# A fused adapter, attention, rotation and mixture-of-experts block on one core: the second norm ahead of the routing, the routing beside the feed-forward products, a reordered opening, and sums moved to ScalarE

## The reference, cut to what matters

```python
B, S, D = 32, 64, 256                      # 2048 tokens
# 1 adapter
hid = gelu(x @ down_W.T + down_b)                       # 64 wide
hid = where(valid, hid @ expert_W[dom].T + expert_b[dom], hid) + domain_emb[dom]
x = layernorm(hid @ up_W.T + up_b + x) * gamma + beta
# 2 attention and feed-forward
x = layernorm(x) * (1 + scale) + shift                  # scale, shift = silu(sin_emb(t)) @ W_ada + b_ada
x = x + softmax(mask(q k^T / 4 + bias)) v @ Wo + bo     # 16 heads of 16
x = x + gelu2((layernorm(x) * g2 + beta2) @ W1 + b1) @ W2 + b2     # 1024 wide
# 3 rotation of pairs by theta and phi of the batch row
# 4 style and mixture of experts
h = layernorm(x) * ln_g + ln_b
h = (h - mean_over_s) * rsqrt(var_over_s) * gamma + beta           # gamma, beta from the subject's style net
gates, idx = top2(softmax(h @ router_w))                # 8 experts, gates normed to sum 1
return x + sum_of_two(gate * (relu(h @ w1[e] + b1[e]) @ w2[e] + b2[e]))
```

## Time and profile before

| | us |
|---|---|
| median of 3 runs | 686.25 (685.91 to 686.96) |
| the profiled execution, its own time | 689.78 |
| its span | 687.9 |
| TensorE, VectorE, ScalarE, GpSimd busy | 557.8, 468.5, 297.2, 226.5 |
| share of the chain that ended last: TensorE, VectorE | 53%, 24% |

### The profile page before, as it was taken

How to read it: one execution, slowest core, us unless ns; L and a number is a source line. 1 busy time by engine, 2 the same in 40 slices (tenths; PEclk the granted TensorE clock), 3 DMA queues, 4 the chain that set the end, 5 groups by cost and what they waited for, 6 DMA issues and landing times.

```text
span 687.9 us, 15375 instructions
## 1 busy us (share of the span) xinstructions
PE 557.8 (81%) x4840; PEld 413.9 (60%) x4841; DVE 468.5 (68%) x1308; ACT 297.2 (43%) x616; POOL 226.5 (33%) x137
## 2 busy tenths in 40 slices
PE   3719576999597997769949399999789999999992
PEld 1616355558385484654838248676567778777771
DVE  5573796689979979883897935886454646474751
ACT  1615542642564425535243232666364444353540
POOL 0412553207714238133370422122612313122222
PEclk9999668999988999989978599999999999999996
DMA  8583451913066451466606576773532322222220
GB/s 288 127 203 124 156 158 56 226 32 123 1 170 160 131 184 63 130 149 227 200 1 244 210 253 232 274 260 49 171 48 41 50 40 42 33 48 38 43 42 0
DMA packets 41176, 86.49 MB, mean 126 GB/s; under 512 B 7321, under 2 KB 31810, under 8 KB 37026
## 3 DMA queue, kind: packets, MB, share of 16 engines
q1 hardware_dynamic: 21744, 56.77, 24.1%
q0 software_dynamic: 8352, 16.99, 13.4%
q10 hardware_dynamic: 11026, 12.02, 5.9%
HBM read 57.23 MB, written 29.44 MB: 126 GB/s over the span
## 4 chain that ended last, share of the span: by engine, by line
PE 53%; DVE 24%; issue 7%; ACT 5%; DMA 5%; ACTq 3%; POOL 2%; SPq 0%; DVEq 0%; POOLq 0%
PE bank L1918 8%; PE bank L1743 6%; PE bank L1907 5%; PE bank L1909 5%; PE bank L1908 4%; PE bank L1919 4%; PE bank L1642 3%; PE bank L1707 2%; PE bank L1723 2%; DMA stage<-in_moe_w 2%; PE bank L1752 2%; PE bank L1697 2%; ACTq L855 2%; DVE stats L1038 2%; DVE sc_sum L1127 2%
## 5 line engine op out<-in xcount | busy, mean ns | idle before, releaser
L1907 PE MATMUL bank<-xs_f,w_moe 128*128 128x128 f16 x624 | 123.3, 221 | 11.0 <-issue 6.6
L1909 PE MATMUL bank<-xs_f,w_moe 128*128 128x128 f16 x624 | 123.6, 221 | 2.7 <-issue 2.7
L867 ACT ACTIVATE stage<-bank,cols 128x128 f32<-128x128 f32 x312 | 88.3, 373 | 81.7 <-PE bank L1909 39.3
L1908 PE MATMUL bank<-xs_f,w_moe 128*128 128x128 f16 x624 | 122.8, 220 | 0.7 <-issue 0.7
L646 POOL DMA_INDIRECT out_x<-x_kept,ids x39 | 62.6, 1606 | 171.3 <-DVE x_kept L1511 122.3
L1907 PEld LDWEIGHTS bank<-xs_f,w_moe 128*128 x624 | 61.1, 98 | 47.0 <-issue 19.2
L1918 PE MATMUL bank<-w_moe,split 128*128 x208 | 79.3, 384 | 0.6
L1908 PEld LDWEIGHTS bank<-xs_f,w_moe 128*128 x624 | 61.4, 98 | 3.6 <-issue 0.8
L1909 PEld LDWEIGHTS bank<-xs_f,w_moe 128*128 x624 | 61.2, 98 | 3.5 <-issue 2.5
L1743 PE MATMUL bank<-w_moe 128*128 128x512 f32 x128 | 59.6, 627 | 3.2 <-ACT w_moe L745 3.2
L1005 DVE SCALAR_TENSOR_TENSOR split<-stage,split 128x2048 f16<-128x2048 f32 x16 | 41.4, 2585 | 30.4 <-ACT split L685 30.4
(11 more groups left out here) (273 smaller groups left out, 1186.8 us busy)
## 6 DMA issues: line engine op xcount, KB each, us to landing
stage<-in_moe_w SPq DMA_DIRECT2D x16, 1024.0 KB, 7.7
w_split<-split SPq DMA_DIRECT2D x16, 1024.0 KB, 4.9
w_moe<-w_split SPq DMA_DIRECT2D x8, 2048.0 KB
w_moe<-in_bias POOLq DMA_DIRECT2D x8, 1024.0 KB, 11.6
xs<-dispatched ACTq DMA_DIRECT2D x41, 130.0 KB
w_moe<-in_x_f SPq DMA_DIRECT2D x4, 512.0 KB, 7.1
w_moe<-in_x_t SPq DMA_DIRECT2D x4, 512.0 KB, 8.0
out_x<-x4b ACTq DMA_DIRECT2D x4, 512.0 KB
```

The lines of the kernel that those rows point to most:

```text
L867: ins = act.activation(h32[j][:, f, :], bank[banks + g][:, P * (f % 4):P * (f % 4) + P], ACT.Relu, bias=moe_b1[:, bass.ds(e, 1), f], scale ...
L1907: pe.matmul(o, hi, xs_f[j][:, k, :], start=(k == 0), stop=False)
L1908: pe.matmul(o, hi, xs_f[j][:, KD + k, :], start=False, stop=False)
L1909: mm = pe.matmul(o, lo, xs_f[j][:, k, :], start=False, stop=(k == KD - 1))
```

## The change

1. Routing a turn later. At the end of a turn TensorE and VectorE no longer run `rank`, `turn_gates`, `expert_biases` and `choose` to `accumulate`. VectorE runs `norm2(c + 1)` right after `style_apply`. The routing of chunk c - 1 runs at the top of turn c, before `norms`; TensorE's three steps stand between the parts of `feed_forward1(c)`, and ScalarE's exponential (`token_gates(c - 1)`) between its second and third activation. `dispatch(c - 1)` moves to the top of GpSimd's turn. The routing of chunk 2 runs beside chunk 3's products, ahead of the plan for the expert stage. Banks are dealt out anew, and the logits are copied by ScalarE (`logits`).
2. Sums to ScalarE. `bo` is added by ScalarE in `keep` (two activations with a bias), the output projection is copied out by ScalarE (`take_x2`), and both halves of `values` are ScalarE's. VectorE's `values` and `residual` are gone.
3. Loop order. `split_low(c + 1, 0)` comes after `sums(0)`; on ScalarE `exponentials(c + 1, 1)` comes after `keys(c + 2)`, and `split_high(c + 1, 2)` after `values`, ahead of `feed_forward_in`; `turn1(c + 2)` comes after the first half of `feed_forward2`, and in turn 1 `scores(c + 1, 1)` after the second.
4. Opening. `ints` and `cols` are loaded first and VectorE starts on them; the other tables come from ScalarE's queue; chunk 0's domain matrices are loaded half by SP and half by ScalarE; `w_qkv` and `main` are issued only after the time angles' activations. The style net runs between the query and key products of chunk 0; `down_projection(1)` and `domain_experts(1)` come before the scores are done; the masks of chunk 1 after both contexts of chunk 0.
5. `x4` is one buffer for all chunks, and `accumulate` adds to it in place.

```diff
 LEFT = 2 + TURNS * STEPS
 ENTRIES = LEFT + STEPS
 DIGIT = E
-ADAPTER_BANKS = ((2, 3, 2), (2, 3, 2), (7, 6, 6), (7, 6, 6))
+ADAPTER_BANKS = ((2, 3, 2), (6, 7, 6), (7, 6, 6), (7, 6, 6))
 TURN1_BANK = (0, 0, 4, 4)
 TURN3_BANK = (4, 4, 4, 6)
-ROUTE_BANK = (0, 0, 0, 3)
-ROWS_BANK = (4, 4, 4, 6)
+LOGIT_BANK = (5, 5, 5, 3)
+COUNT_BANK = 3
+ROWS_BANK = (2, 2, 2, 6)
 GATES_BANK = (2, 2, 2, 3)
 B2_BANK = (2, 2, 2, 6)
...
-    load_x(0)
-    load_x(1)
+    load_features(0)
+    sp.dma_start(down_w[:], t["down_w"].rearrange("(k p) a -> p k a", p=P)).then_inc(down_in, 16)
+    load_experts(0, CB // 2)
+    load_tokens(0)
+    load_features(1)
+    load_experts(1)
     load_part(0, 0)
+    load_tokens(1)
...
     for c in range(NCH - 1):
         residual(c)
-        confirm(c)
+        if c > 0:
+            dispatch(c - 1, range(TT))
         less_maximum(c + 1, 0)
         if c + 2 < NCH:
             shift_norm(c + 2)
@@ -629,12 +629,13 @@
         probabilities(c + 1, 0)
         rotate_odd(c)
         probabilities(c + 1, 1)
+        confirm(c)
         if c + 3 < NCH:
             select(c + 3)
         if c + 2 < NCH:
             add_bias(c + 2)
-        dispatch(c, range(TT))
     residual(NCH - 1)
+    dispatch(NCH - 2, range(TT))
     confirm(NCH - 1)
...
+    for dst, src in early:
+        act.dma_start(dst[:], src).then_inc(early_in, 16)
+    for dst, src in of_adapter:
+        act.dma_start(dst[:], src).then_inc(adapter_in, 16)
...
+
+    act.wait_ge(dom_ready, 1)
+    _, chosen = nc.values_load_multi_w_load_instructions(
+        dom_at[0:1, CB // 2:CB], engines=[mybir.EngineType.Activation], min_val=0, max_val=NDOM - 1)
+    for b in range(CB // 2):
+        act.dma_start(w_raw[:, CB // 2 + b, :],
+                      t["exp_w"][bass.ds(chosen[b], 1), :, :].rearrange("e a o -> a (e o)")
+                      ).then_inc(w_raw_in.sem, 16)
+    act.dma_start(w_ada[:], t["w_ada"].rearrange("(k p) n -> p k n", p=P)).then_inc(ada_in, 16)
+    for dst, src in of_style:
+        act.dma_start(dst[:], src).then_inc(style_in, 16)
...
+    act.dma_start(w_qkv[:], t["w_qkv"].rearrange("(k p) n -> p k n", p=P)).then_inc(qkv_in, 16)
+    for dst, src in main:
+        act.dma_start(dst[:], src).then_inc(main_in, 16)
+
+    act.wait_ge(mask_ready, 1)
+    for u in range(2):
+        mask(0, u)
+    split_high(0, 0)
+    queries(0)
+    keys(0)
+    split_high(0, 1)
+    values(0)
+    hidden(1)
...
-    act.wait_ge(mask_ready, 1)
-    for u in range(2):
-        mask(0, u)
-    act.wait_ge(main_in, N_MAIN)
-    split_high(0, 0)
-    queries(0)
-    keys(0)
-    values(0)
     keep(0)
-    split_high(0, 1)
+    split_high(0, 2)
     exponentials(0, 0)
-    hidden(1)
     exponentials(0, 1)
-    split_high(0, 2)
     context(0, 0)
+    context(0, 1)
     mask(1, 0)
-    context(0, 1)
+    take_x2(0)
     mask(1, 1)
-    split_high(0, 3)
     queries(1)
     keys(1)
     keep(1)
 
     hidden(2)
     values(1)
+    split_high(0, 3)
     for c in range(NCH - 1):
         feed_forward_in(c)
+        feed_forward(c, range(2))
         if c > 0:
-            feed_forward(c, range(5))
+            token_gates(c - 1)
+        feed_forward(c, range(2, KF))
+        if c > 0:
+            store(c - 1)
             split_high(c, 3)
-            feed_forward(c, range(5, KF))
-        else:
-            feed_forward(c, range(KF))
+        exponentials(c + 1, 0)
         split_high(c + 1, 0)
-        exponentials(c + 1, 0)
-        split_high(c + 1, 1)
-        exponentials(c + 1, 1)
         if c + 2 < NCH:
             queries(c + 2)
             keys(c + 2)
+        exponentials(c + 1, 1)
         context(c + 1, 0)
+        split_high(c + 1, 1)
         norm3(c)
         context(c + 1, 1)
         if c + 2 < NCH:
-            for u in range(2):
-                mask(c + 2, u)
-        split_high(c + 1, 2)
-        token_gates(c)
+            mask(c + 2, 0)
+        take_x2(c + 1)
+        if c + 2 < NCH:
+            mask(c + 2, 1)
+        logits(c)
         rows(c)
         if c + 3 < NCH:
             hidden(c + 3)
         if c + 2 < NCH:
             keep(c + 2)
             values(c + 2)
-        store(c)
+        split_high(c + 1, 2)
...
-    dve.wait_ge(cond_in, N_COND)
+    dve.memset(v_bd[:], 0.0).then_inc(zeroed, 1)
+    step(dve.tensor_scalar(bq4[:], bq[:], 0.25, None, ALU.mult))
+    step(dve.tensor_tensor(bkp[:], bk[:].unsqueeze(2).broadcast_to([P, KD, 2]),
+                           parity[:].unsqueeze(1).broadcast_to([P, KD, 2]), ALU.mult))
+    dve.wait_ge(early_in, N_EARLY)
+    dve.tensor_copy(ident16[:], ident[:]).then_inc(zeroed, 1)
+    dve.tensor_copy(lower16[:], lower[:]).then_inc(zeroed, 1)
+    dve.wait_ge(setup_pe, 1)
+    step(dve.tensor_copy(add_o[:], bank[7][0:A, 0:B]))
+    dve.wait_ge(zeroed, 9)
+    hidden()
+    dve.wait_ge(adapter_in, N_ADAPTER)
+    residual()
+    norms()
+    dve.wait_ge(setup_pe, 2)
+    for m in range(2 * KD):
+        step(dve.tensor_scalar(ada[:, m, :], bank[5][:, B * m:B * m + B], b_ada[:, m:m + 1],
+                               1.0 if m < KD else 0.0, ALU.add, ALU.add))
+    dve.drain().then_inc(cond_ready, 1)
+    scale_norm()
...
+    split_low(0, 0)
...
-    dve.wait_ge(setup_pe, 6)
+    split_low(0, 1)
...
+    scores(0)
+    hidden, adapter_residual, norms = adapter(1)
+    hidden()
+    scores(1)
+    adapter_residual()
+    sums(0)
...
+    sums(1)
     norms()
+    split_low(0, 2)
+    stages = second_half(0)
+    norm2, *_ = stages
+    scale_norm, *_ = attention(1)
     scale_norm()
...
-    split_low(0, 0)
-    values()
-    scores(0)
-    split_low(0, 1)
-    scores(1)
-    hidden, adapter_residual, norms = adapter(1)
-    hidden()
-    sums(0)
-    adapter_residual()
-    sums(1)
-    split_low(0, 2)
-    norms()
-    stages = second_half(0)
-    residual, norm2, *_ = stages
-    residual()
-    scale_norm, *_ = attention(1)
-    scale_norm()
-    split_low(0, 3)
...
     for c in range(NCH - 1):
-        _, values, scores, sums = attention(c + 1)
-        (_, _, second_residual, rotate, norm3, style_stats, style_scale, style_apply, choose,
-         token_gates, find_place, copy_gates, accumulate, fill_rows) = stages
-        values()
+        _, scores, sums = attention(c + 1)
+        if c + 2 < NCH:
+            hidden, adapter_residual, norms = adapter(c + 2)
+            hidden()
+        if c == 0:
+            split_low(0, 3)
+        else:
+            fill_rows()
+            choose()
+            token_gates()
+            find_place()
+            copy_gates()
+            split_low(c, 2)
         if c + 2 < NCH:
             adapter_residual()
+        if c > 0:
+            accumulate()
+        if c + 2 < NCH:
             norms()
         if c > 0:
             split_low(c, 3)
...
-        split_low(c + 1, 0)
         scores(1)
         sums(0)
+        split_low(c + 1, 0)
+        (_, second_residual, rotate, norm3, style_stats, style_scale, style_apply, choose,
+         token_gates, find_place, copy_gates, accumulate, fill_rows) = stages
...
-        residual, norm2, *_ = stages
-        residual()
-        choose()
-        token_gates()
-        find_place()
-        copy_gates()
-        fill_rows()
+        norm2, *_ = stages
         norm2()
-        accumulate()
-        if c + 3 < NCH:
-            hidden, adapter_residual, norms = adapter(c + 3)
-            hidden()
-        split_low(c + 1, 2)
...
+    split_low(NCH - 1, 2)
+    fill_rows()
+    choose()
+    token_gates()
+    find_place()
+    copy_gates()
     plan_early()
+    accumulate()
...
+    pe.wait_ge(early_in, N_EARLY)
+    pe.wait_ge(setup, SETUP_DOM)
+    pe.matmul(bank[7][0:A, 0:B], dom_emb[:], hot_dom[:], start=True, stop=False)
+    pe.matmul(bank[7][0:A, 0:B], exp_b[:], hot_val[:], start=False, stop=True).then_inc(setup_pe, 1)
+    domain_experts(0)
+    pe.wait_ge(zeroed, 9)
+    pe.wait_ge(adapter_in, N_ADAPTER)
+    up_projection(0)
+    pe.wait_ge(ada_in, 16)
     pe.wait_ge(setup_act, 4)
...
-    domain_experts(0)
-    pe.wait_ge(zeroed, 9)
-    up_projection(0)
     turn1(0)
     pe.wait_ge(cond_ready, 1)
-    pe.wait_ge(main_in, N_MAIN)
-    queries(0)
-    keys(0)
+    pe.wait_ge(qkv_in, 16)
+    pe.wait_ge(x1_ready.sem, x1_ready.of(0, 2))
+    project(0, 0, wq, q_done, range(0, 1))
+    pe.wait_ge(style_in, N_STYLE)
+    pe.wait_ge(setup, SETUP_SUB)
+    pe.matmul(bank[4][0:SE, 0:B], subj_emb[:], hot_sub[:], start=True, stop=True).then_inc(setup_pe, 1)
+    project(0, 0, wq, q_done, range(1, KD))
+    pe.wait_ge(setup, SETUP_SE)
+    pe.matmul(bank[5][0:SH, 0:B], hyp_w1[:], se[:], start=True, stop=True).then_inc(setup_pe, 1)
+    project(0, 2, wk, k_done, range(0, 1))
+    pe.wait_ge(setup, SETUP_SE + 1)
+    pe.matmul(bank[6][0:SH, 0:B], hyp_w2[:], hyp1[:], start=True, stop=True).then_inc(setup_pe, 1)
+    project(0, 2, wk, k_done, range(1, KD))
+    pe.wait_ge(setup, SETUP_SE + 2)
```

(38 more changed lines are left out.)

214 lines of the change are left out of this document (93 added, 121 removed).

## The result

| | before | after |
|---|---|---|
| first comparison, median of 4 runs each | 686.4 | 680.9 (676.6 to 682.1) |
| a profiled execution, own time (span) | 689.78 (687.9) | 682.14 (680.3) |

The ratio is 0.991 (95% interval 0.989 to 0.993), 5.5 us gained where 12.4 were forecast. That is not all of the result: the same changed kernel, measured twice more later, stood at 1.003 (1.000 to 1.007) and 1.005 (1.001 to 1.009) of the kernel before, which took 692.1 and 691.6 beside it. The gain was there in one measurement of three. The ratios leave out runs more than 1.5% above the kernel's fastest; over all twelve runs of each, the two later medians are 697.8 and 698.8, which is 5.8 and 7.2 above the kernel before.

The account below looks back on a forecast made before the run. Stages bound it: TensorE waits for VectorE's routing and norm, the two alternate in S to O, and the opening is a lone chain. 10.8 + 20.0 - 16.5 - 1.9 = 12.4 us gained, median 686.25 to 674, range 665 to 684.

Parts of the forecast that it names:

- O to S: From a turn's first routing product (O) to the next turn's first feed-forward product (S): 20.0 us gained over three turns.
- the stop of 2.3 ahead of `turn_gates`: In chunks 1 to 3, TensorE stops 2.3 us within the feed-forward products, waiting for the gates.
- that rival: A table load costs twice its 1.28 us: gates and stop come 1.3 later, 3.9 in three chunks; 678, chance 0.03.
- The opening: From the start to chunk 0's first feed-forward product: 10.8 us gained (9.9 + 2.9 - 2.0), bounds 6 and 14.
- S to O: From a turn's first feed-forward product to its first routing product, three times: 16.5 us lost together, 10 to 20.
- the handover: From chunk 3's first feed-forward product to the first expert product, 31.09 us before: 1.9 lost, 0 to 4.
- Step (b): Turns 1 and 2: routing beside feed-forward products stops TensorE 2.3 us and puts VectorE's norms 10 later, 5 to 6 absorbed.
- (c): In S to O, `split_low(c + 1, 0)` now lies ahead of the third norm: 2.5 us in the sum.
- (a): Turn 0's S to O, without routing: `exponentials(1, 1)` waits for ScalarE's keys, `sums(1)` 3.5 us later, 1 to 4.
- Expert stage: From the first expert product to the end of the span, 263.0 us: taken as untouched and costed at nothing.
- the cases at 680 and 681: 680: the opening gains 5 instead of 10.8, chance 0.19. 681: the norm ahead gains 2 instead of 5.5 each, 0.09.
- the slower one: Routing beside the products holds VectorE until each S to O grows more than it saves, by 11.5: 692, chance 0.07.

Follow-up runs that it names:

- routing-back kernel: Changed kernel with all engines' routing steps back between the router and the next chunk's second norm, other changes kept: 1.005 of before.
- fillers: Changed kernel with ten useless products (128x512 or 128x128) in TensorE's stop ahead of `turn_gates`, turns 1 and 2: 1.010 and 1.009 of before.
- e6: Changed kernel with the gap's exponential ahead of the first `feed_forward` activation (chunk 3: behind the first): 0.987 of before.
- e12: Changed kernel with the gates' activation ahead of the first `feed_forward` activation and computed in the same table as these: 0.979 of before.
- e5: Changed kernel with `split_low(c + 1, 0)` back ahead of `scores(1)` and `split_high(c + 1, 0)` ahead of the exponential: 1.001 of before.
- e2: Changed kernel with `turn_gates` two feed-forward parts later and `expert_biases` one part later in TensorE's queue: 1.004 of before.
- e7: Changed kernel with ten useless 128x128 products in TensorE's stop ahead of `turn_gates` in turns 1 and 2: 1.009 of before.

## Why the prediction was wrong in size

**Right.** Direction and range of the first measurement; the bottleneck by stages; the opening's chain (first query product 39.65, forecast 41; chunk 1's 101.52, forecast 105; first feed-forward product 119.89, forecast 125); O to S, 20.6 of 20.0, with 13.7, 11.7 and 8.8 where 14, 12 and 9 stood; the two loads inside the products and the stop of 2.3 ahead of `turn_gates` (2.27, 2.26, 2.26). On the load itself the Trainium skill ("ScalarE: Activation LUTs", What ACT_TABLE_LOAD costs) has 1.28 and a drain of 1.38 behind it. The trace has the 1.28, with the exponential 1.29 after the load's start, and no drain; that rival is out.

**The opening** gave 15.9 instead of 10.8, more than its upper bound of 14. Both first parts were shorter than I took: chunk 0's queries 11.1 earlier (9.9), the stretch to chunk 1's 5.3 shorter (2.9), and ScalarE's longer part cost 0.5 and not 2.0. (The 4.4 of the masks and the shift should have been 4.5, from 2.46 and 2.09.)

**The term that failed is S to O with the handover**: 18.4 lost in the sum, 31.3 in the trace. The routing-back kernel splits it.

- *Step (b) and the handover, the routing beside the products: 9.9 forecast (4.5, 3.5, 1.9, with 2.5 for (c) taken off the 7 and 6), 17.0 measured (5.6, 5.0, 6.4).* I placed the second activation's end at S + 4.35 and the gates at S + 7.8, with every part at 1.74, the full clock's price. In turn 1 it was S + 6.1 and S + 9.5: behind the pause ahead of S (1.56, 4.57, 0.87 in the three) the clock was already halved, and in turn 1 and chunk 3 it halved again behind the stop. `feed_forward1` with its routing steps took 21.1, 20.6 and 21.8 where the sum has 17.4, from 13.90, 1.2 and 2.3. The rows before had it: rows 1 show 15.89 and 15.83 beside 13.90 for the same products, and I carried that as a slow start that may stay, not as the price of a pause that I was about to add three times. (The row behind the pause of 2.10 has 14.00, though: even there the price was not paid each time.) The fillers show the price, e6 and e12 that it is gone with the stop. How much of S to O's growth is these slow products and how much is VectorE's wait of 7.30 and 9.69 for the exponential isn't told apart.
- *Steps (a) and (c), and what else is changed in the loop: 8.5 forecast (3.5, 2.5, 2.5), 14.3 measured (5.1, 6.1, 3.5, handover 0.4 less).* It lies where GpSimd's `probabilities(c + 1, 0)` takes 5.67 instead of 3.62 beside `split_low`, and TensorE waits 4.74 and 6.79 for it. e5 says that the position of `split_low` is at most 3 of this; the rest isn't attributed.

**Handover.** 37.1 instead of 33.0: `feed_forward1` with its routing steps took the 21.8 instead of 17.4. The order of rows and store, which the sum doesn't have, was harmless here by 1.3 us; in e2 and e6, and in the third measurement's trace of the changed kernel itself, it was not.

**Expert stage.** 2.4 gained in the first pair, with nothing changed in it; over all traces here it lies between 260 and 267, so this is no effect of the change that I could show.

**Not foreseen at all** is what the later traces show: the routing a turn later brings the scatters from the long products to the short ones. No term of mine priced pauses of TensorE beside GpSimd's transfers. Where they appear the whole change is worth nothing, in two measurements of three, though the opening's 16 us are there in all. That they appeared in every later trace with scatters beside short products and in none of the early ones is not explained.

**Rivals.** In the first measurement the cases at 680 and 681 come nearest by number and neither by its mechanism: the opening gave 15.9, not 5, and S came as early as the forecast had it. In the later traces the slower one comes closest, in part by its own: its point was a growth of S to O of 9.6 on average, and it is 5.2, 17.4 and 10.1 there, mean 10.9; the larger gain of the opening is what keeps the whole near zero.

**A version that beats both** is e12: 0.979 of before in two measurements, 677.4 and 676.0.

## What to carry to other kernels

Price a new stop of TensorE as the stop and, as an upper bound, the slower products behind it, and read that price from places in the trace where the same products start after a pause. Then ask whether the turn waits for these products at all. When a small step of one engine is put between the steady work of another, put it where its input is ready, ahead of the queue's next wait, not behind two items of it. And when work is moved in time, move its transfers in the sum too: ask which products they will run beside, and which other transfer they are issued just ahead of or just behind.

## What the hardware showed that was not expected

- Pauses as short as 1.0 us in the scores, or 1.56 ahead of S, were followed by a granted clock of 0.50; but not always: behind the same 1.55 to 1.57 us the first eight products took 5.40 (after), 5.25 (e7) and 3.70 (e12), and behind stops of 2.3 in the products eight took 5.40 in 15 cases and 3.70 in 8.
- TensorE pauses by 0.4 to 2.6 us a turn, with nothing to wait for that the profile shows, where 64 short products run beside indirect scatters; in ten later traces with that overlap always, in four early ones never, and not beside the output store alone.
- Loads of 130 KB of rows, issued 1.5 us behind a store of 1 MB and beside loads of 2 MB, made TensorE wait 8.33 us; 0.6 to 0.8 behind it 2.25 to 3.01; issued 0.9 to 1.4 ahead of it, nothing.
- The kernel before took 686.4, 686.8, 690.0, 692.1, 691.6 and 691.6 in six measurements, the changed one 0.991, 1.003 and 1.005 of it. My expectations put that down to the chip; no run shows that it is, and one and the same chip had 686.8 in one measurement and 691.6 in another. Small verdicts need both kernels in one measurement, and more than one of these.
